# Two of eight adjacency blocks moved from the rank stage into the search of the hard rows, and 24 instead of 32 candidates sorted

## The reference

```python
def _top_p_attention(X, W1, W2, W3):
    q = X @ W1.T @ W2.T
    k = X @ W3.T
    probs = jax.nn.softmax(q @ k.T, axis=-1)
    idx = jnp.argsort(-probs, axis=-1)
    sp = jnp.take_along_axis(probs, idx, axis=-1)
    keep_sorted = jnp.cumsum(sp, axis=-1) - sp < 0.9
    A = probs * (keep_sorted scattered back by idx)
    return A / A.sum(-1, keepdims=True)

R = adj + I;  R = R / R.sum(-1, keepdims=True)
Xf = Xa = x;  Z = 0
for n in range(2):
    Xf = R @ Xf
    Xa = _top_p_attention(Xa, W1, W2, W3) @ Xa
    Z = Z + Xf @ U1[n].T + Xa @ U2[n].T
out = layernorm(x + layernorm(x + Z) * ln_g + ln_b)
```

## Time and profile before

| what | value |
|---|---|
| time, median of 3 runs | 1803.95 us (1803.54 to 1804.17) |
| the profiled execution's own time | 1805.14 us |
| its span in the profile | 1803.5 us |
| TensorE busy | 1542.5 us (86%) |
| VectorE busy | 1352.3 us (75%) |
| ScalarE busy | 786.6 us (44%) |
| GpSimd busy | 229.5 us (13%) |
| mean granted clock of TensorE | 0.922 |

### The profile page before, as it was taken

The page is one execution under the profiler, slowest core; times in us unless marked ns, Lnnn a source line. Parts: engine busy times, 40 slices in busy tenths (PEclk is TensorE's granted clock), DMA queues, the critical chain, the costliest instruction groups (busy, mean ns, idle before and its releaser), DMA issues. The chain is left out here.

```text
span 1803.5 us, 18434 instructions
## 1 busy us (share of the span) xinstructions
PE 1542.5 (86%) x4753; PEld 890.1 (49%) x4753; DVE 1352.3 (75%) x3836; ACT 786.6 (44%) x1246; POOL 229.5 (13%) x264
## 2 busy tenths in 40 slices
PE   6999999941599999998999999992247878988995
PEld 3555555521355555554565565661224534544553
DVE  4677777756567777776799999994768888887652
ACT  3444444421355555555444444441223334334443
POOL 1011111123000000000011111112010131211223
PEclk9999999975699999999999999996568998899997
DMA  7556666600235555555556766640000000000000
GB/s 246 187 190 195 196 190 187 188 24 1 94 140 192 197 194 195 198 202 219 184 169 184 187 174 178 172 155 3 2 2 1 1 7 6 1 6 7 7 6 12
DMA packets 52365, 211.89 MB, mean 117 GB/s; under 512 B 21760, under 2 KB 30528, under 8 KB 31664
## 3 DMA queue, kind: packets, MB, share of 16 engines
q1 hardware_dynamic: 49008, 210.56, 36.4%
q0 software_dynamic: 3264, 0.30, 0.2%
HBM read 206.63 MB, written 4.45 MB: 117 GB/s over the span
## 5 line engine op out<-in xcount | busy, mean ns | idle before, releaser
L1527 DVE MAX8 cand<-psL 128x8 f32<-128x256 f32 (+1 forms) x640 | 372.5, 584 | 92.6 <-PE psL L775 85.2
L1104 ACT ACTIVATE psL<-psL,umax 128x1024 f32<-128x1024 f32 x256 | 278.6, 1088 | 326.3 <-DVE umax L1521 317.4
L774 PE MATMUL psL<-kA,mq 128*128 128x512 f32 x512 | 298.7, 583 | 7.6 <-DVE mq L1354 7.6
L893 PE MATMUL psO<-ebuf,xn 128*128 128x512 f32 x512 | 241.8, 594 | 0.0
L752 PE MATMUL psO<-adj_in,xn 128*128 128x512 f32 x512 | 241.1, 595 | 0.0
L752 PE MATMUL psO<-adj_in,xf 128*128 128x512 f32 x512 | 241.0, 595 | 0.0
L1788 DVE SCALAR_TENSOR_TENSOR ebuf<-ebuf 128x1024 f32<-128x1024 f32 x128 | 156.7, 1225 | 100.1 <-PE psO L893 93.6
L1233 ACT ACTIVATE ebuf<-psL 128x1024 f32<-128x1024 f32 x128 | 129.8, 1021 | 194.0 <-PE psL L951 138.7
L775 PE MATMUL psL<-kB,mq 66*128 66x512 f32 x512 | 203.7, 398 | 0.0
L1170 ACT ACTIVATE ebuf<-psL 128x1024 f32<-128x1024 f32 x128 | 131.0, 1023 | 137.0 <-PE psL L865 137.0
L963 PE MATMUL psO<-xf,xa 128*128 128x512 f32 x340 | 171.7, 629 | 17.4 <-DVE xf L1995 17.4
(11 more groups left out here) (354 smaller groups left out, 2073.5 us busy)
## 6 DMA issues: line engine op xcount, KB each, us to landing
adj_in<-in_adjT SPq DMA_DIRECT2D x128, 1024.0 KB, 4.8
adj_in<-in_adj SPq DMA_DIRECT2D x32, 2048.0 KB, 7.7
xaT<-in_xT SPq DMA_DIRECT2D x1, 2048.0 KB, 7.8
xa_dram<-xa SPq DMA_DIRECT2D x8, 256.0 KB, 7.8
out<-t SPq DMA_DIRECT2D x8, 256.0 KB, 2.3
list_dram<-ids,place POOLq DMA_INDIRECT x64
rel_prob<-cut_dram SPq DMA_DIRECT2D x32, 2.0 KB
cut_dram<-ncut SPq DMA_DIRECT2D x16, 2.0 KB
```

The costliest lines, as they stand in the source:

```text
L774: nc.tensor.matmul(o, qA[:, t * P:(t + 1) * P], kA[:, c:c + BI], start=True, stop=False)
L893: last = nc.tensor.matmul(psO[:], xs[:, j, :], ekept[:, u % 2, hb * BI:(hb + 1) * BI], start=(j == 0), stop=(j == JT - 1))
L1104: nc.scalar.activation(ps[:], ps[:], ACT.Exp, bias=umax[:, bass.ds(i * UB + k, 1)], scale=1.0, accum_out=usum[:, bass.ds(i * UB + k, 1)]). ...
L1527: last = v.max(cand[:, t % 2, at + c * 8:at + c * 8 + 8], psL[(turn + k) % 3][:, c * WIDE:(c + 1) * WIDE])
```

## The change

The first step alone is changed, and in it:

- TOPS[0] is 24 instead of 32: 24 of the 32 candidates of a row are sorted.
- The rank stage multiplies FLOWS = 6 of the 8 adjacency blocks, spread evenly over its 128 units: `flow_window(a)` gives block a 21 or 22 units, the first of which has no adjacency matmul; `ROWS_AT` and `OVER_AT` say in which unit a finished block is transposed and copied.
- Block 6's first 8 matmuls stand before `ranks(7)`, the next 16 after `to_rows(5)`, the last 8 after the logits of the first tile of hard rows. Block 7's 32 follow, then the loop.
- `add_self(6)` and `add_self(7)` on POOL stand between `gather(0)` and the loop.
- SP's loads are one list of 64, with the stores of the cuts between them.
- The tile's exponentials lie in `xa` (free in the first step until the mix) instead of in adj_in, and there is one buffer for them instead of two. So the next tile's logits and exponentials come after h_mid, and VectorE's `prepare(c + 1)` after the flag.
- SP waits for the 64th use of adj_in before the mix stage's first load.

```diff
-    TOPS = [32] + [64] * (STEPS - 1)
+    TOPS = [24] + [64] * (STEPS - 1)
+        first_exp = xa[:].rearrange("p t d -> p (t d)")
+        FLOWS = 6
+        def flow_window(a):
+            return a * NB * UB // FLOWS, (a + 1) * NB * UB // FLOWS
+        def flow_parts(unit):
+            a = next(b for b in range(FLOWS) if unit < flow_window(b)[1])
+            first, end = flow_window(a)
+            before = max(unit - first - 1, 0) * JT // (end - first - 1)
+            return a, range(before, max(unit - first, 0) * JT // (end - first - 1))
+        def flow_rows(a):
+            end = flow_window(a)[1]
+            fitting = [unit for unit in range(end + 1, NB * UB) if 4 <= unit % UB <= 8]
+            return fitting[0] if fitting else None
+        ROWS_AT = {flow_rows(a): a for a in range(FLOWS) if flow_rows(a) is not None}
+        OVER_AT = {flow_window(a)[1] - 1: a for a in range(FLOWS)}
...
+                if s == 0:
+                    for n in range(NB * PARTS):
+                        flow_load(n)
+                        if n >= 12 and n % FLOWS == 0 and (n - 12) // FLOWS < NB:
+                            rank_store((n - 12) // FLOWS)
...
+                SELF_BEFORE = {0: (0, 1), 1: (2,), 2: (3,), 4: (4,), 5: (5,)}
...
                     gather(0)
+                    for a in range(FLOWS, NB):
+                        add_self(a)
                     with pool.Fori(0, tiles) as c:
                         pool.wait_ge(g["h_x"], c * 48 + 48)
...
+                            if s == 0:
+                                a, flow = flow_parts(i * UB + k)
+                                if a > 0 and i * UB + k == flow_window(a)[0] + 1:
+                                    pe.wait_ge(g["r_o_sb"], a)
+                                for j in flow:
+                                    adj_part(a, j)
...
                 pe.wait_ge(g["st_tally"], NB - 1)
+                if s == 0:
+                    pe.wait_ge(g["r_o_sb"], FLOWS)
+                    for j in range(0, JT // 4):
+                        adj_part(FLOWS, j)
                 ranks(NB - 1)
                 pe.wait_ge(g["st_tally"], NB)
                 if s == 0:
-                    to_rows(NB - 1)
+                    to_rows(FLOWS - 1)
+                    for j in range(JT // 4, FLOWS * JQ):
+                        adj_part(FLOWS, j)
...
-                    pe.wait_ge(g["r_n_sb"], NB)
-                    prepare(0)
+                    pe.wait_ge(g["r_n_sb"], FLOWS)
+                    prepare_q(0)
+                    prepare_logits(0)
+                    for j in range(FLOWS * JQ, JT):
+                        adj_part(FLOWS, j)
+                    for a in range(FLOWS, NB):
+                        pe.wait_ge(g["r_o_sb"], a + 1)
+                        to_rows(a)
+                        if a + 1 < NB:
+                            for j in range(JT):
+                                adj_part(a + 1, j)
+                    pe.wait_ge(g["r_n_sb"], NB)
                     with pe.Fori(0, tiles) as c:
-                        prepare(c + 1)
+                        prepare_q(c + 1)
                         pe.wait_ge(g["h_flag"], c + 1)
                         nc.tensor.matmul(psS[:, 0:1], ones[:], hflag[:], start=True, stop=True).then_inc(g["h_flags"], 1)
                         pe.wait_ge(g["h_mid"], c + 1)
+                        pe.wait_ge(g["h_exp"], c * NU + NU)
+                        prepare_logits(c + 1)
...
-                    prepare(0)
+                    prepare_q(0)
+                    prepare_exp(0)
+                    for a in range(FLOWS, NB):
+                        rank_o_copy(a)
+                        rows_copy(a)
                     with act.Fori(0, tiles) as c:
-                        prepare(c + 1)
+                        prepare_q(c + 1)
...
+                        prepare_exp(c + 1)
...
-                        weights = rowexp[:, bass.ds(turn, 1), 0:N].rearrange("p o a -> p (o a)")
+                        weights = first_exp
...
                         settle_chord()
-                        prepare(c + 1)
                         below(weights, rest)
...
                                                op0=ALU.is_lt, op1=ALU.mult).then_inc(g["h_flag"], 1)
+                        prepare(c + 1)
```

More of the change, by code:

```diff
@@ L327, in slot @@
             return k * units // 16
+        FLOWS = 6
[12 more added lines that the diff above has]
+        OVER_AT = {flow_window(a)[1] - 1: a for a in range(FLOWS)}
+        assert len(ROWS_AT) == FLOWS - 1 and len(set(unit // UB for unit in ROWS_AT)) == FLOWS - 1
         def sweep_slots():
@@ L401, in rank_store, with flow_load @@
                                          src[:, rows]).then_inc(g["cut_out"], 16)
[L403 to L409, removed]
+                def flow_load(n):
+                    if n >= RING:
+                        sp.wait_ge(g["adj_used"], n - RING + 1)
+                    sp.dma_start(adj_in[:, n % RING], adjT[n // PARTS, :, bass.ds(n % PARTS * JQ, JQ), :]).then_inc(g["adj_in"][n % RING], 16)
+                if s == 0:
[3 more added lines that the diff above has]
+                            rank_store((n - 12) // FLOWS)
+                else:
+                    rank_loads(0, True)
+                    rank_loads(1, False)
+                    with sp.Fori(2, NB) as i:
+                        rank_loads(i, False)
+                        rank_store(i - 2)
+                    rank_store(NB - 2)
+                    rank_store(NB - 1)
                 def mix_loads(i, first):
@@ L438, in _ @@
                     mix_loads(1, False)
+                    sp.wait_ge(g["adj_used"], NB * PARTS)
                     natural_loads(0, True)
@@ L534, in _ @@
                 assert JQ == TB and PARTS == NB
-                add_self(0)
+                SELF_BEFORE = {0: (0, 1), 1: (2,), 2: (3,), 4: (4,), 5: (5,)}
+                if s > 0:
+                    add_self(0)
                 for i in range(NB):
-                    if i < RING - 1:
-                        add_self(i + 1)
-                    if s > 0:
+                    if s == 0:
+                        for a in SELF_BEFORE.get(i, ()):
+                            add_self(a)
+                    else:
+                        if i < RING - 1:
+                            add_self(i + 1)
                         add_x(i, 0)
-                    if RING - 1 <= i < NB - 1:
-                        add_self(i + 1)
-                    if s > 0:
+                        if RING - 1 <= i < NB - 1:
+                            add_self(i + 1)
                         add_x(i, 1)
@@ L737, in rank_q, with adj_part @@
                     nc.tensor.matmul(psQ, wq[:], xaT[:, cols(i)], start=True, stop=True).then_inc(g["r_q_ps"], 1)
+                def adj_part(i, j):
+                    r = j // JQ
+                    if j % JQ == 0:
+                        pe.wait_ge(g["adj_in"][r % RING], (i * (PARTS // RING) + r // RING) * 16 + 16)
+                        if r == i:
+                            pe.wait_ge(g["self_in"], (i + 1) * TB)
+                    last = nc.tensor.matmul(psO[:], fs[:, j, :], adj_in[:, r % RING, j % JQ, :],
+                                            start=(j == 0), stop=(j == JT - 1))
+                    if j % JQ == JQ - 1:
+                        last.then_inc(g["adj_used"], 1)
                 def rank_block(i, prev, more, turn):
@@ L744, in adj_with @@
                         return range(sum(counts[:k]), sum(counts[:k + 1]))
[L746 to L755, removed]
                     if prev is None:
@@ L780, in rank_block @@
                                     pe.wait_ge(g["r_q_lo2"], i + 1)
-                                if s == 0 and k == slot(4, UB):
-                                    to_rows(prev)
+                                if s == 0 and i * UB + k in ROWS_AT:
+                                    to_rows(ROWS_AT[i * UB + k])
                                 if s > 0 and k == slot(3, UB):
@@ L788, in rank_block @@
                                     if s == 0:
-                                        pe.wait_ge(g["r_n_sb"], prev + 1)
+                                        if len([n for n in ROWS_AT if n < i * UB + k]) > 0:
+                                            pe.wait_ge(g["r_n_sb"], len([n for n in ROWS_AT if n < i * UB + k]))
                                     else:
@@ L792, in rank_block @@
                                     ranks(prev)
[L794 to L800, removed]
+                            if s == 0:
[4 more added lines that the diff above has]
+                                    adj_part(a, j)
+                            else:
+                                if k == 1:
+                                    if prev is not None:
+                                        pe.wait_ge(g["r_o_sb"], i)
+                                    else:
```

(7 more changed lines are left out.)

17 lines of the change are left out of this document (9 added, 8 removed).

## The result

The changed kernel takes 1789.7 us (1787.79 to 1791.29, 4 runs) against 1803.74 us (four runs of the kernel before; 1803.95 was the median of three): a ratio of 0.9922, interval 0.991 to 0.9935. It is 14.0 us faster. The profiled execution took 1791.29 us, its span 1789.7.

The account below looks back on a forecast made before the run. TensorE was taken to bound the rank stage, a serial chain the tail and search. Terms -53.7 - 1.0 + 0.2 + 2.0 + 27.7 + 0.1 = -24.7 us took the median 1803.95 to 1779, range 1771 to 1793.

Parts of the forecast that it names:

- Rank stage: -53.7: First step's rank stage: moving blocks 6 and 7 off TensorE saves 56.2 us at most, 53.7 after 2.5 for waits.
- the five waits in mid-block: Rank stage: TensorE waits for psO's copy at five new places, 0.5 us each, 2.5 in all, bounds 0 and 10.
- Rival (a): Rank stage: VectorE becomes the bound; plausible form costs 9 us, giving 1788. Chance 0.10.
- The search starts late ... +27.7: Search start: h_ref waits behind add_self(6), add_self(7) and load 63; 27.7 us later, bounds +26 and +32.
- Rival (c): Search: it overlaps all the moved work, so the 27.7 us delay is missing, giving 1752. Chance 0.03.
- Rival (e): Tail and search: moved matmuls run at half clock; the 24 on the path take 20.6 us more, giving 1800. Chance 0.03.
- Three hops by 0 to 2.7 us ... I take 2: Tail: POOL's list scatter, gid read and gathers slowed beside 1 MB loads; 0 to 8.1 us, 2 taken.
- rival (b): Tail: small transfers queue behind four loads, 14 us a hop, 42 in all instead of 2, giving 1819. Chance 0.05.
- -1.0 ... + 0.2: Tail after the rank stage: VectorE's shorter sorting and statistics save 1.0 us; matmuls before the rank sums cost 0.2.
- Search to mix: Search end to mix: later logits and query move cost 1.6 us, TensorE's earlier activity returns 1.5; +0.1 in all.
- More hard rows? ... 0: Hard-row tiles: sorting 24 leaves the same 48 hard rows, one tile and no second; 0 us.
- the first search pass: Sign at the search start: the first pass starts about 67 to 70 us after the rank stage's end.

Follow-up runs that it names:

- e1: Changed kernel with POOL's wait for h_x and three copies ending in h_ref moved ahead of add_self(6) and add_self(7): 1762.62 us, ratio 0.9776.
- e4: Changed kernel with the edits of e1 and e2 together, nothing further: 1748.51 us, ratio 0.9697.
- e2: Changed kernel: loads from 52 held until first gather landed, cuts' last store before them, 16 block-6 matmuls after the tile's logits instead of 8: 1783.62 us.
- e6: Changed kernel with the last store of the cuts ahead of load 52 instead of behind load 54, no load held: 1784.67 us, ratio 0.9903.
- e7: e4 with the loads from 52 on held only until the scatters have landed, instead of the gather: 1753.09 us, ratio 0.9725.

## Why the prediction was right, and where it failed

- **"Rank stage: -53.7."** Right: -54.7. The cost of one matmul, 0.86 us, gave the size. The 2.5 us set aside for the five waits in mid-block were too much: the stage came within 1.5 us of the bound of 56.2. Rival (a) did not happen: TensorE was busy for 297.99 of 298.56 us.
- **"The search starts late ... +27.7."** Right, to 0.1 us, and the wait is shown by e1, where h_ref was taken from behind the last load and 27.1 us went. Some luck is in the last digit: from the end of the logits to hupper it took 29.4 us instead of 29.8 (377.05 to 406.48), and the tile's logits took 0.5 more than before (6.62 against 6.16). Half of what the first term gained was given back here. One count beside the sum was wrong: 48 matmuls ahead of the search and 16 beside it. While load 63 lands and POOL adds and copies (399.3 to 406.5), TensorE goes on, so 56 lie ahead and only 8 beside, at a granted clock of 1.00 (406.48 to 413.03). Rival (c), the overlap that the change speaks of, did not come about in the changed kernel; e1 and e4 are what it looks like when made.
- **The clock.** Rival (e) fell: the 8 matmuls straight behind the tile's logits (377.13, 16 records) took 7.03 us at a granted clock of 1.00. The tile's logits themselves had 0.54, after TensorE had stood idle for 16.71 us. The rule of the Trainium skill (TensorE: Matmul & The Clock Gate, Part 1: The HAM clock gate), half rate by default and full rate by activity, agrees with both rows; it did not price the moved work, since that came in one piece.
- **"Three hops by 0 to 2.7 us ... I take 2": the step that failed.** Measured were 8.3 us on the scatters (12.88 - 4.56), 3.2 on gid (5.56 - 2.32) and 0 on the gathers, 11.6 in all, above the term's own upper bound of 8.1. That small transfers queue beside the loads was named, as the unknown and as rival (b); neither size, 2 in all or the rival's 14 a hop, was met. The gathers cost nothing for the reason that was given: from 363 to 368 us the ring was full and the DMA engines stood at 0.03. Three errors lie in the size.
  - The bound of 2.7 us was read from a row that does not hold the case. The earlier trace rows has nine landings: two stores of 35 KB at 16 us (the 4.9 is one of them), two reads of gid in the idle stretches, and five reads in the second step, from 1254.9 us on. None of the 64 scatters has a landing in it, and nothing between 60 and 380 us, the loaded stage.
  - The rank stage is no measure of the tail either: its DMA engines stood at 0.60 on average, those of the tail at 1.00 from 330 to 341 us.
  - The store of the cuts was moved behind three loads into the midst of the scatters (341.63 us; they run from 339.24 to 344.04). Its cost was counted only as its own lateness ("about 4 us later"), which indeed cost nothing, and not as traffic that others wait behind. Against the quiet case of e2 the two waits are 13.6 us too long; the store's place is worth 6.1 of them by e6, and 7.5 go when the loads are held too, with the reservation made there.

  The rule of the Trainium skill that was cited (DMA: Bandwidth & Descriptors, Queues, rings and completion order) pointed to the upper bound of 8.1; the measured 11.6 lies even above it, and on the last hop the term was 0.
- **"-1.0 ... + 0.2."** The way from the stage's end to the first scatter grew by 1.2 us (13.84 against 12.62) instead of shrinking by 0.8. The rank sums stand behind matmuls that wait 1.82 us for their load, and VectorE waited 2.1 us for the sums. That load stands in SP's queue behind the store before the last, of 318.50 us; the two loads issued between 322 and 334 us took 10.9 and 13.8 us to land. The text had said that stores ahead of loads cost nothing with four buffers; in the stage that was so, at its end not.
- **Search to mix, "+0.1".** Measured +1.3: the way to the mix's first matmul cost 1.8 (59.81 against 58.02 us; 1.6 was forecast), and of the 1.5 taken back only 0.5 came. The mix still began at a granted clock of 0.57 (6.92 us for its first records against 7.38), although TensorE had worked until 3.19 us before it.
- **"More hard rows? ... 0."** Right: one tile, and no fallback.
- **"1779 ... 1771 to 1793."** The range holds the result because the terms beside the transfers nearly cancelled (-0.7) and the range was wide: the failed term alone, 9.6 us over the 2 taken, used most of the 14 us above the forecast. Of the signs named, the first search pass came 82.0 us after the stage's end (407.44) instead of 67 to 70, much the same miss.

## What to carry to other kernels

Work moved beside a serial chain is free only if nothing of the chain stands behind it on any queue: read each engine's program in order, and look for a semaphore that a short step raises behind a long wait (here 0.2 us of copying behind 35.7 us of waiting). Short copies that release another engine go first. Bulk loads and element-wise stores are kept away from a chain of small dependent transfers: in e4, where the loads were held for some 18 us, the search still set the end, and letting them go earlier (e7) was 4.6 us slower. And before a bound is read from a view of landings, look which transfers it counts, and when they ran.

## What the runs showed of the hardware

- Small transfers beside bulk loads: a read of 1 KB took 2.3 us without loads, 4.0 (e6) to 6.1 us (e7) beside them. POOL's wait behind four list scatters was 2.5 us with no load in flight (e2, e4; DMA engines at 0.02 in e2), 4.6 in the kernel before, 8.4 with loads and the store 5 us ahead of the first scatter (e6), 12.9 with loads and the store among the scatters. Why the quiet case before the change (4.56) is slower than that of e2 (2.55) was not tried by itself; the store is 2 us ahead of the scatters there, 5 us in e2, which fits.
- Behind a store of 512 pieces of 4 bytes and two of 128 pieces of 16 bytes, the loads' rate fell from 410 GB/s to 78 (changed kernel) and 25 (e6) for 6 us and more. The reason is open.
- POOL beside VectorE: four additions of 128x128 took 1.7 us alone, 4.0 in e4 and 10.1 in e1 beside VectorE's passes with two SBUF inputs; the issue of one gather of 128 rows took 1.0 us alone and up to 4.9 beside them. VectorE's own pass stayed at 4.48 to 4.57 us.
